# The pair mask of a self attention, added by sixteen 32x32 tiles of TensorE's array

## The reference

```python
def _attn(q, k, v, mask):
    scale = 1.0 / np.sqrt(HD)
    s = jnp.einsum('bqhd,bkhd->bhqk', q, k) * scale
    s = jnp.where(mask, s, jnp.finfo(s.dtype).min)
    a = jax.nn.softmax(s, axis=-1)
    return jnp.einsum('bhqk,bkhd->bqhd', a, v)
```

## Time and profile before

| | |
|---|---|
| time, median of 3 runs | 1566.06 us (1566.05 to 1567.51) |
| the profiled execution | 1563.82 us, of which the span 1562.2 us |
| mean granted clock of TensorE | 0.953 |
| TensorE busy over the span | 86% |
| self attention, first to last L431 | 146.9 to 570.4 us |
| one group of eight slots of it | 26.86 us |

### The profile page before, as it was taken

One profiled execution on the slowest core, in us unless ns is written; L12 is line 12 of the kernel. 1 busy time (PEld: TensorE's weight loads), 2 busy tenths in 40 slices (PEclk: granted clock), 3 DMA queues, 4 the chain that ended last, 5 costly groups with the idle time before them and its releaser, 6 DMA issues. The chain is left out here.

```text
span 1562.2 us, 44242 instructions
## 1 busy us (share of the span) xinstructions
PE 1337.8 (86%) x17952; PEld 746.4 (48%) x17952; DVE 805.7 (52%) x1772; ACT 905.3 (58%) x1692; POOL 688.2 (44%) x1405
## 2 busy tenths in 40 slices
PE   2584999999999988499999998889987488888885
PEld 2531555555555442255555555334433355555563
DVE  4263565656665546255555554522167355565553
ACT  0171555555555547277777777644476477777773
POOL 0004556565656520466666663001100566666640
PEclk9996999999999999699999999899998799999996
DMA  2502534344343500444444442000000555555423
GB/s 82 151 1 54 101 64 92 73 84 82 73 92 63 102 2 1 87 89 84 83 84 83 81 83 37 0 0 0 0 1 1 99 93 100 95 96 92 89 46 108
DMA packets 136124, 103.44 MB, mean 66 GB/s; under 512 B 13913, under 2 KB 135666, under 8 KB 135922
## 3 DMA queue, kind: packets, MB, share of 16 engines
q1 hardware_dynamic: 135922, 100.62, 32.8%
HBM read 9.08 MB, written 4.19 MB: 8 GB/s over the span
## 5 line engine op out<-in xcount | busy, mean ns | idle before, releaser
L535 DVE TENSOR_REDUCE negmax<-ps_nat 128x8 f32<-128x616 f32 (+1 forms) x384 | 361.1, 940 | 403.8 <-PE ps_nat L442 159.9
L624 ACT ACTIVATE p<-ps_st 128x1024 f32<-128x1024 f32 (+1 forms) x256 | 260.5, 1018 | 181.5 <-PE ps_st L472 179.5
L489 PE MATMUL ps_po<-p,vz 77*32 77x128 f32 (+1 forms) x6144 | 248.5, 279 | 26.6 <-issue 24.6
L431 PE MATMUL ps_nat<-stacks 64*128 64x77 bf16 (+1 forms) x3072 | 134.2, 209 | 58.0 <-DMA stacks<-parts 51.7
L667 POOL TENSOR_TENSOR ot<-vv,den 128x256 f32<-128x256 f32 x192 | 139.5, 727 | 100.4 <-ACT den L616 99.3
L465 PE MATMUL ps_st<-stacks 64*77 64x128 bf16 (+1 forms) x3072 | 158.0, 223 | 24.7 <-ACT p L624 22.4
L489 PEld LDWEIGHTS ps_po<-p,vz 77*32 77x32 f32 (+1 forms) x6144 | 145.9, 109 | 64.2 <-issue 29.9
L624 ACT ACTIVATE p<-ps_st,key_bias 77x1024 f32<-77x1024 f32 x128 | 141.5, 1105 | 59.9 <-PE ps_st L472 59.7
L653 POOL CAST nm<-negmax 128x32 bf16<-128x32 f32 x192 | 40.0, 209 | 289.9 <-DVE negmax L535 289.8
L431 PEld LDWEIGHTS ps_nat<-stacks 64*128 64x128 bf16 x3072 | 78.1, 97 | 179.3 <-issue 147.0
L679 POOL TENSOR_TENSOR whole<-whole,parts 128x512 f32<-128x512 f32 x96 | 98.3, 1024 | 137.4 <-ACT parts L587 137.4
(11 more groups left out here) (142 smaller groups left out, 2144.0 us busy)
## 6 DMA issues: line engine op xcount, KB each, us to landing
stacks<-parts SPq DMA_DIRECT2D x512, 128.0 KB, 3.2
stacks<-parts SPq DMA_DIRECT2D x256, 77.0 KB, 2.6
p<-in_x_dram SPq DMA_DIRECT2D x16, 256.0 KB
out_dram<-p SPq DMA_DIRECT2D x16, 256.0 KB, 2.4
p<-in_ctx_dram SPq DMA_DIRECT2D x16, 154.0 KB
ht<-in_L_xcond_adaLN_W_dram SPq DMA_DIRECT2D x1, 576.0 KB
w<-in_L_xcond_mlp_W_dram SPq DMA_DIRECT2D x2, 256.0 KB
wqkv<-in_L_xcond_qkv_W_dram SPq DMA_DIRECT2D x1, 192.0 KB
```

Of the source, the lines that this page charges most:

```text
L431: m = t.matmul(c.ps_nat[h][:, nk * g:nk * g + nk], qst[half(h), par, at, S * j:S * j + S], kst[half(h), par, at, nk * j:nk * j + nk], star ...
L489: m = t.matmul(bank[32 * g:32 * g + 32, S * p:S * p + S], c.vz[0:nk, i % 2, j, g, 32 * hh:32 * hh + 32], c.p[0:nk, hh, S * g:S * g + S], s ...
L535: v.tensor_reduce(c.negmax[:, step % 2, 8 * p:8 * p + 8].rearrange("p (h g) -> p h g", h=2), c.nat_pair[:].rearrange("p (h n) -> p h n", h ...
L624: a.activation(c.p[0:nk, 2 * p:2 * p + 2, :].rearrange("p h n -> p (h n)"), c.st_pair[0:nk, :], ACT.Exp, bias=bias).then_inc(exped, 1)
```

## The change

The two mask matmuls of `natural` and the two of `transposed` are removed. A new step `masks(u)` at the head of the slot, after `turn_max(u // 2)`, starts all four banks instead: the two of `ps_nat` for unit `u + 3` and the two of `ps_st` for unit `u`. Each bank gets four matmuls with 32x32 weights, one for each 32 output partitions `q`, taken from tile row `(q + b) % 4` of the array for bank `b`; together they use each of the 16 tiles once, with 512 moving columns each. A matmul contracts over the partitions of its tile row, so the mask rows have to lie on those partitions: `rolled` holds four copies of the mask (two plain, two transposed), each with its blocks of 32 rows rotated by `b`. They are written in the set-up by 16 transfers on SyncE's queue, which wait for `mask_t`, and SyncE waits for their landing before the block ends. The waits for the reduction (`maxed`) and for the exponential (`exped`) move to the head of the slot, in front of all sixteen. `nat_full` is now signalled by the last L431 of each bank. The cross attentions keep their code.

```diff
+            sp.wait_ge(masks, 2)
+            for b in range(4):
+                mask = c.mask_nat if b < 2 else c.mask_t
+                for q in range(4):
+                    r = 32 * ((q + b) % 4)
+                    sp.dma_start(c.rolled[r:r + 32, b, :], mask[32 * q:32 * q + 32, :]).then_inc(rolled, 16)
+            sp.wait_ge(rolled, 16 * 16)
...
-            v.tensor_copy(c.mask_t[:], c.turned_mask[:, 0:S])
+            v.tensor_copy(c.mask_t[:], c.turned_mask[:, 0:S]).then_inc(masks, 1)
...
+            def masks(u):
+                nat, st = in_range(u + AHEAD), in_range(u)
+                if nat and u + AHEAD > 0:
+                    pe.wait_ge(maxed, u + AHEAD)
+                if st and u > 0:
+                    pe.wait_ge(exped, u)
+                banks = [(b, c.ps_nat[b]) for b in range(2) if nat] + [(2 + b, c.ps_st[b]) for b in range(2) if st]
+                for q in range(4):
+                    for b, bank in banks:
+                        r = 32 * ((q + b) % 4)
+                        t.matmul(bank[32 * q:32 * q + 32, :], c.eye_bf[r:r + 32, r:r + 32],
+                                 c.rolled[r:r + 32, b, :].unsqueeze(1).broadcast_to([32, 4, S]),
+                                 start=True, stop=False, skip_group_check=True)
...
-                if u > 0:
+                if u > 0 and not pair_mask:
                     pe.wait_ge(maxed, u)
...
-                                     start=g == 0, stop=g == 3, skip_group_check=True)
-                        if g == 3 and not (pair_mask or key_mask):
+                                     start=g == 0 and not pair_mask, stop=g == 3, skip_group_check=True)
+                        if g == 3 and not key_mask:
                             m.then_inc(nat_full, 1)
...
-                    if pair_mask:
-                        t.matmul(kept, c.eye_bf[:], c.mask_nat[:].unsqueeze(1).broadcast_to([128, 4, nk]),
-                                 start=False, stop=True, skip_group_check=True).then_inc(nat_full, 1)
...
-                if u > 0:
+                if u > 0 and not pair_mask:
                     pe.wait_ge(exped, u)
-                if pair_mask:
-                    for h in range(2):
-                        t.matmul(c.ps_st[h][0:nk, :], c.eye_bf[:], c.mask_t[:].unsqueeze(1).broadcast_to([128, 4, S]),
-                                 start=True, stop=False, skip_group_check=True)
...
+                if pair_mask and (in_range(u) or in_range(u + AHEAD)):
+                    masks(u)
+        c.rolled = sb("rolled", [128, 4, S], BF16)
```

More of the change, by code:

```diff
@@ L84, in setup_phase @@
                                                  s("su_silu_d"), s("su_copied"))
-    made, masks, mask_ps = s("su_made"), s("su_masks"), s("su_mask_ps")
+    made, masks, mask_ps, rolled = s("su_made"), s("su_masks"), s("su_mask_ps"), s("su_rolled")
     steps, cleared = s("su_steps"), s("su_cleared")
```

## The result

The change gains 7 us, a sixth of the 45 that were forecast. The kernel after takes 1559.18 us (median of 8 runs, 1550.42 to 1563.23) against 1566.35 (8 runs, 1564.10 to 1568.03) on the same chip: a ratio of 0.9949, 95% interval 0.9929 to 0.997. The forecast was 1521.5. The profiled execution took 1558.07, with a span of 1556.2 against 1562.2.

A forecast was written before the change was run, and what follows sets the result against it. The self attention was taken as bound by what TensorE streams. Savings of 45.1 us and 0.5 for the set-up gave 1563.8 - 45.1 + 0.5 = 1519.2 profiled, 1521.5 as median with 2.2 added; range 1498 to 1558.

The forecast's parts named there:

- M: At each slot's head: time of the sixteen mask tiles with the shape change behind them, 0.41 us, bounds 0.31 to 0.98.
- The rounds of four: Rival: only one tile row writes a bank at a time, so the masks take 0.98 us; total 1585, chance 0.11.
- Wait 1: Slots 4 and 6: the next masks wait for ScalarE's exponential, losing 0.64 us each, 1.28 per group.
- T + 2.09: End of VectorE's reduction, 2.09 us after the masks' start T; claimed a lesser wait than the exponential's end at T + 2.36.
- Wait 2: Slots 1, 3 and 7: L450 waits for the copy before the transpose, losing 0.17, 0.17 and 0.14 us, 0.48 per group.
- Wait 3: Slot 5: L431 waits for the stacked keys' transfers, losing about 0.4 us per group, between nothing and 0.8.
- The clock: Rival: TensorE's clock falls by half for long stretches because it pauses in every group; chance 0.06 together with no overlap.
- The sum: Self attention: groups 1 to 13 save 39.6 us, group 0 2.0, group 14 2.7, group 15 0.8; 45.1 in all.
- The set-up: The 16 rolled-copy transfers on SyncE's queue, mostly hidden by the modulation's products, add 0.5 us, between nothing and 2.

The follow-up runs named there:

- experiments 1 and 4: 1: changed kernel, later groups reading the first group's stacked queries and keys, 1511.29 us; 4: changed kernel, queries' and keys' middle splits done earlier, 1516.04 us.
- experiment 6: The kernel before the change with only the queries' and keys' middle splits done earlier, no tiles or rolled copies: 1561.92 us, ratio 0.9978.
- experiment 8: The changed kernel without the stacked queries' transfers for groups after the second, keys' transfers and wait kept: 1546.86 us, ratio 0.9882.

## Why the prediction was wrong

**M, the sixteen tiles: right.** Forecast 0.41, measured 0.37, all starts within 0.05 instead of 0.11. The bounds had reached to 0.98.

**The rounds of four: refuted.** The four tiles of one bank come from four tile rows, and all sixteen start within 0.05 us; rounds would have needed 0.98. The rule of the Trainium skill (TensorEngine Tiling (Array Packing), "Gotcha 1: PSUM Pressure") that speaks for that rival doesn't hold in this measurement, where the tile rows write different rows of the bank.

**Wait 1, the exponential: right in size, half right in its cause.** 1.30 and 1.31 from L507 to the next masks in slots 6 and 4 against 1.22; without a wait for the keys these slots stay at 2.45. But behind slot 6 the profile names VectorE's reduction in 12 of 14 groups:

```profile
412.82 0.39 PE L440 MATMUL ps_nat<-rolled,eye_bf 32*32 32x512 bf16 x2 [0.66 <-DVE negmax L555]
```

The forecast had that wait end at T + 2.09, 0.27 ahead of the exponential's. It left out that VectorE first takes in slot 5's projection (L577, 410.43 to 411.56), so that the reduction begins at 411.48 and ends at 412.69. The exponential ends at 412.68. By these two ends a faster exponential alone would gain nothing in slot 6.

**Wait 2, the copy: right.** L472 starts at 421.50, 0.15 behind the end of the copy (L565) at 421.35, as forecast. Slots 1, 3 and 7 take 3.02 to 3.07; 3.54 less 0.65 with 0.17 lost is 3.06. All eight slots of a group come to 23.28 where the keys are in time (experiments 1 and 4); the forecast's 23.8 less its 0.4 is 23.4.

**Wait 3, the stacked keys: the step that failed.** The mechanism was named, on the right instruction and in the right slot, but it was sized at 0.4 with a bound of 0.8, and it is 1.95. The working had the last landing at T0 + 15.0 (T0, the start of slot 0's masks, lies 0.60 ahead of the point from which the table counts, by the forecast 0.65). It adds "0.2" for the queries, which "end almost where these begin". They end 0.7 later than the keys could begin. Before, the queries' last issue was done at 4.68 and the keys' split at 5.44, a gap of 0.76. The keys' chain starts from slot 0, but the queries' from slots before it, and these got shorter: the first query issue moved from 1.03 ahead of slot 0's scores to 0.23 ahead, and the eight issues now take 6.37 instead of 5.71. "Keep their pace" was true neither of their start nor of their duration. The landing was taken as the median 3.2; the scores start 3.70 behind the last issue, against the 3.40 of the groups without an instruction load near it. And the lengthening by instruction loads was not in the sum at all.

In the forecast's terms the keys were to be there at T0 + 15.0, and the scores of slot 5 start at T0 + 16.4 (15.83 and the 0.60 from the masks to L483). The first key issue makes 0.5 of this (6.8 instead of 6.3), the span of the eight issues 0.4 (5.88 instead of 5.48), issue to scores 0.5 (3.70 instead of 3.2); the scores were also due 0.15 earlier than forecast. From the means of the traces the wait (15.83 against 13.85 due) adds up like this: 0.52 with the queue free, the issues' span as before (5.52) and 3.40 to the scores; 0.79 by the later first issue; 0.36 by the longer span; 0.30 by the later landings.

**The clock: a case not priced.** The forecast put the fallen clock among the rivals only for "long stretches". It fell for 3.4 us at a time (once 6.8), in 8 of 13 groups, and each behind one of the waits for the keys. That is 1.1 per group, 14 us in all, and it makes a wait of 1.95 cost 3.04. Before, the trace already had the pattern at its one long wait, with the slot behind it on a fallen clock; the forecast used that only for a gain.

**The sum.** For groups 1 to 13 the forecast saved 39.6; they saved 7.1 (13 x 0.545). Group 0 saved 2.1 (forecast 2.0), group 14 1.6 (2.7), the rest 0.8 (0.8). Together 11.5 instead of 45.1, to rounding. The line view gives the first and last start of the transposed scores before and after, 421.7 apart and 410.2 apart:

```profile
L465 PE MATMUL ps_st<-stacks x1024: 215/217/313, 158.3 to 580.0; 64*128 64x128 bf16 x171
```

```profile
L483 PE MATMUL ps_st<-stacks x1024: 216/216/311, 158.5 to 568.7; 64*128 64x128 bf16 x171
```

**The set-up: mis-sized.** Forecast 0.5 with an upper bound of 2; it holds the next block's first load up by 3.9. The price of 0.34 per issue came from loads of the earlier trace rows that come from DRAM; these go from SBUF to SBUF, and one starts every 0.63. It reaches the scores: the first natural scores start at 149.8 instead of 146.9, and over the profiled executions at 148.7 to 151.7 in the five kernels with sixteen transfers, but at 145.4 to 147.1 in the three with seven and at 144.8 and 146.9 in the two with none. The first transposed scores start only 0.2 later than before, since the slots ahead of them, with natural scores alone, got 2.7 shorter; the forecast had no term of its own for those. The spans then add up: 2.9 - 2.7 - 11.5 + 5.3 = -6.0.

**What stays open.** Behind the last scores the profiled execution is 5.3 us longer than that of before (1556.2 - 568.7 against 1562.2 - 580.0, to 0.1), in code that is the same. In the kernels of the experiments the same stretch takes 984 to 995, against 982 before. In experiment 6, which has no tiles, it takes 993; so most of the scatter isn't due to this change. What sets it was not tried. That instruction loads lengthen issues and landings rests on where they fall together in the traces: there was no run with the same timing and fewer loads. Why a group with a longer pause may keep its clock while one with a shorter loses it is open too.

## What to carry to other kernels

When a change shortens a loop on the bounding engine, write down for every transfer chain in it from which slot it starts and in which it is needed, and recompute the gaps between chains that share a queue: two chains tied to different slots close up, and the queue turns their overlap into lateness. Count the latest of a set of transfers, not the median, and add what a pause costs on top of itself: here a wait of 2 us cost 3. If a faster piece brings little, look for the one wait that ate it and move its producer earlier; the order that was worth 4 us before the change was worth 40 after it.

## What the runs showed of the hardware that was not expected

- Sixteen matmuls of 32x32 tiles with 512 columns start within 0.05 us, four of them into different rows of each of four banks, and are through in 0.37 with the change of shape. Eight of 64x64 take 0.56.
- DMA issues of 1.0 to 1.9 us on SyncE's queue, where others take 0.54 to 0.9, go with a load of instructions (16 KB on q8, 0.9 to 1.6 us) that begins within 0.7 us of their start: 10 of 10 long issues before, 25 of 25 after, 13 of 13 in experiment 8. Of the issues with a load that near 48 of 84 are long, of the 444 others none. Twelve more matmuls in each of the eight slots of a group brought 0.77 more such loads per group.
- An SBUF to SBUF transfer of the set-up takes SyncE's queue 0.59 us to issue for 32 rows as for 96, and the next starts 0.63 behind it. The loads from DRAM on the same queue take 0.25 to 0.60 each, the eight of the earlier trace rows 0.34.
- The granted clock fell from 1.00 to 0.50 (2.4 to 1.2 GHz) for 3.4 us behind two pauses of 0.66 and 1.10 us with 0.4 us of work between them. It did so in 8 of 13 groups; in the other five, whose second pauses were 1.11 to 1.77, it stayed.
